# First half on one core: features as sixteen 32x32 tiles over head pairs, and a bias add that moves ahead of a norm's scaling

## The reference

```python
def favor(x, omega):                       # omega: 16 x 8
    xs = x * dh ** (-0.25)                 # dh = 16
    u = jnp.einsum('bshd,dm->bshm', xs, omega)
    h = 0.5 * jnp.sum(xs * xs, axis=-1, keepdims=True)
    return jnp.concatenate([jnp.exp(u - h), jnp.exp(-u - h)], axis=-1) * m ** (-0.5)
...
q, k, v = (out @ W[l] + b[l] for each of q, k, v), in 16 heads of 16
Qf, Kf = favor(q, omega[l]), favor(k, omega[l])
a = causal_linear_attention(Qf, Kf, v) @ Wo[l] + bo[l]
h = layer_norm(out + a, ln1_g[l], ln1_b[l])
y = relu(h @ W1[l] + bf1[l]) @ W2[l] + bf2[l]
out = layer_norm(h + y, ln2_g[l], ln2_b[l])
```

## Time and profile before

| what | value |
|---|---|
| median of the runs | 2623.1 us (3 runs, 2620.6 to 2625.83) |
| the profiled execution | 2624.48 us, its span 2622.7 us |
| PE, share of the span busy | 97% |
| DVE, ACT, POOL | 81%, 59%, 54% |
| mean granted clock of TensorE | 0.993 |
| largest step of the chain that ended last | PE, 90% |

### The profile page before, as it was taken

How to read it: one execution, slowest core, us unless ns; L and a number is a source line. 1 busy time by engine, 2 the same in 40 slices (tenths; PEclk the granted TensorE clock), 3 DMA queues, 4 the chain that set the end, 5 groups by cost and what they waited for, 6 DMA issues and landing times.

```text
span 2622.7 us, 63564 instructions
## 1 busy us (share of the span) xinstructions
PE 2545.6 (97%) x22368; PEld 2096.2 (80%) x22368; DVE 2119.8 (81%) x5244; ACT 1545.4 (59%) x3137; POOL 1423.9 (54%) x1406
## 2 busy tenths in 40 slices
PE   7899999999999999999898999999999999999998
PEld 4688888888888888887776788888888887888876
DVE  5788877887777787888899888878898887888775
ACT  3544455445544554455246777777777777776772
POOL 2244344443444345445476756656676666776664
PEclk9999999999999999999999999999999999999999
DMA  3100000010000010000111100000111100110001
GB/s 91 38 18 10 18 2 17 14 36 2 1 2 13 15 39 10 18 26 25 52 38 56 29 17 12 19 16 14 35 32 35 31 27 23 35 32 27 28 29 48
DMA packets 78985, 67.32 MB, mean 26 GB/s; under 512 B 15800, under 2 KB 73272, under 8 KB 78680
## 3 DMA queue, kind: packets, MB, share of 16 engines
q1 hardware_dynamic: 78680, 63.25, 8.1%
HBM read 49.18 MB, written 12.58 MB: 24 GB/s over the span
## 4 chain that ended last, share of the span: by engine, by line
PE 90%; DVE 4%; issue 3%; ACT 2%; POOL 1%; SPq 0%; DMA 0%; DVEq 0%; ACTq 0%; POOLq 0%
PE PS L274 79%; PE PS L984 4%; PE PS L946 1%; PE PS L1014 1%; PE PS L937 1%; PE PS L487 1%; PE PS L477 1%; PE PS L425 1%; PE PS L895 1%; DVE PS L3586 1%; DVE U L3178 1%; PE PS L1044 0%; ACT PR L2246 0%; DVE SQ L3566 0%; SPq L5388 0%
## 5 line engine op out<-in xcount | busy, mean ns | idle before, releaser
L2246 ACT ACTIVATE PR<-PS,SM 128x256 f32<-128x256 f32 (+1 forms) x512 | 280.3, 559 | 136.5 <-DVE SM L3591 136.0
L1932 ACT ACTIVATE FB<-PS,BC 128x512 f32<-128x512 f32 x192 | 133.4, 695 | 323.0 <-PE PS L274 184.7
L3178 DVE TENSOR_TENSOR U<-PS,CST 128x512 f32<-128x512 f32 x384 | 238.2, 683 | 34.2 <-PE PS L274 33.9
L4618 POOL TENSOR_TENSOR RL<-FB,RH 128x512 fp32r<-128x512 f32 x96 | 126.0, 1312 | 219.9 <-DVE RH L3155 219.9
L274 PE MATMUL PS<-W2H,RH 128*128 128x256 f32 x768 | 226.1, 294 | 6.7 <-POOL RL L4618 6.6
L4840 POOL TENSOR_TENSOR SM<-SM,COL 128x8 f32<-128x8 f32 x128 | 223.8, 1748 | 10.7
L3586 DVE CUSTOM_DVE_ANT_0 PS<-PS,MSK 128x256 f32<-128x256 f32 (+1 forms) x512 | 202.6, 436 | 29.4 <-PE PS L274 28.2
L274 PE MATMUL PS<-W2H,RL 128*128 128x256 f32 x768 | 215.9, 281 | 0.0
L274 PE MATMUL PS<-W2L,RH 128*128 128x256 f32 x768 | 215.8, 281 | 0.0
L4630 POOL TENSOR_TENSOR SBD<-SBD,TMP 128x256 f32<-128x256 f32 x84 | 64.3, 766 | 207.3 <-DVE TMP L3170 207.3
L274 PEld LDWEIGHTS PS<-W2H,RH 128*128 128x128 f32 x768 | 145.1, 189 | 29.5 <-issue 24.9
(11 more groups left out here) (265 smaller groups left out, 8535.6 us busy)
## 6 DMA issues: line engine op xcount, KB each, us to landing
PX<-in_L_attn_x SPq DMA_DIRECT2D x16, 512.0 KB, 3.6
TB<-in_k_rot SPq DMA_DIRECT2D x64, 128.0 KB, 2.1
SG<-in_L_attn_W SPq DMA_DIRECT2D x24, 256.0 KB, 2.7
xp_scratch<-PX SPq DMA_DIRECT2D x8, 512.0 KB, 2.9
xs_scratch<-X SPq DMA_DIRECT2D x64, 64.0 KB, 1.5
ZS<-xs_scratch SPq DMA_DIRECT2D x16, 256.0 KB, 2.8
GG<-xp_scratch SPq DMA_DIRECT2D x7, 512.0 KB, 3.8
out<-GG SPq DMA_DIRECT2D x7, 512.0 KB, 2.9
```

What stands on the lines that cost most here:

```text
L1932: e.activation(FB[:, hb % 2, :], PS[:, 5, :], ACT.Relu, bias=BC[:, l % 2, 4 + hb:5 + hb]).then_inc(*a_re.up(n, hb))
L2246: t = e.activation(PR[:, par, 256 * i + lo:256 * i + hi], PS[:, 3 + par, 256 * i + lo:256 * i + hi], ACT.Exp, bias=S[:, 40 + 2 * g + i:41 ...
L3178: e.tensor_tensor(heads(U[:, u % 6, :], 4), heads(PS[:, g, :], 4), bcast(CM, 4), ALU.mult).then_inc(*d_mk.up(n, u))
L4618: e.tensor_tensor(RL[:, r, :], FB[:, 0, :], RH[:, r, :].bitcast(F), ALU.subtract).then_inc(*p_rl.up(n, hb))
```

## The change

**Columns.** The 16 heads are dealt out over the projected tiles in pairs. Each of the four tiles now holds, in its four groups of 32 partitions, a pair of heads of the keys or the queries, so that `proj(n, i)` needs the weights of both and splits of them are written with a stride. **Operands.** ACT writes the columns with their bias to one full tile and the squares to another, with two activations of 128 x 512 for each i. **Visit.** `favor(n)` is one visit of 32 matmuls of 32 rows x 32 columns x 512: for each bank r and each operand c one with the omega weights, and then for each r and c one with the constant weights of the squares that adds to it. Rows 32r to 32r+31 of operand c go to partitions 32c to 32c+31 of bank r. It waits for all four operands and for both `add_bv(n, 0)` and `add_bv(n, 1)`. **Order.** On PE `values(n, 1)` moves ahead of `up(m, 2)` and `down(m, 1)`; on DVE `add_bv(n, 1)` moves ahead of `norm2_b(n - 3)` (in the stages 22 and 23 the order on DVE stays). **Loads.** The bias columns take four transfers instead of two per layer, `features_of` one operation of 128x32 instead of two of 128x128. `load_scales(0)` moves on SP ahead of the last loads of the first half, `load_scales(1)` to the start of the second half, and `table(u)` waits for the first six transfers alone while u < 32. For this GG, G0 and QSB lie elsewhere in SBUF.

```diff
         def proj(n, i):
-            m, nm = i % 2, "wk" if i < 2 else "wq"
...
-            need_weights(e, piece_of(n // 8, nm))
+            if i == 0:
+                need_weights(e, piece_of(n // 8, "wq"))
+                need_weights(e, piece_of(n // 8, "wk"))
...
-        def favor(n, i, bank):
+        def favor(n):
             l = n // 8
-            e.wait_ge(*p_om.at(l, 1))
-            e.wait_ge(*a_sq.at(n, i))
-            if i < 2:
-                e.wait_ge(*a_sq.at(n, 2 + i))
-            else:
-                e.wait_ge(*d_v.at(n, i - 2))
-            mm(e, PS[0:64, bank, :], OM[:, l % 2, 0:64], OPS[i][0], True)
-            mm(e, PS[64:128, bank, :], OM[:, l % 2, 64:128], OPS[i][1], True).then_inc(*e_fv.up(n, i))
+            e.wait_ge(*p_om.at(l))
+            for i in range(4):
+                e.wait_ge(*a_sq.at(n, i))
+            for i in range(2):
+                e.wait_ge(*d_v.at(n, i))
+            for r in BANKS:
+                for c in range(4):
+                    mm(e, PS[32 * c:32 * c + 32, r, :], OM[32 * r:32 * r + 32, l % 2, 0:32], OPS[c][0][32 * r:32 * r + 32, :], True)
+            for i, r in enumerate(BANKS):
+                for c in range(4):
+                    t = mm(e, PS[32 * c:32 * c + 32, r, :], HO[32 * r:32 * r + 32, 0:32], OPS[c][1][32 * r:32 * r + 32, :], False)
+                t.then_inc(*e_fv.up(n, i))
...
             values(n, 0)
             down(m, 0)
+            values(n, 1)
             up(m, 2)
             down(m, 1)
-            values(n, 1)
-            favor(n, 0, 2)
-            favor(n, 1, 3)
-            favor(n, 2, 0)
-            favor(n, 3, 1)
+            favor(n)
...
         def operands(n, i):
...
-            e.activation(A[lo, :], PS[lo, i, :], ACT.Identity, bias=col[lo, :])
-            e.activation(B[hi, :], PS[hi, i, :], ACT.Identity, bias=col[hi, :])
-            e.activation(A[hi, :], PS[lo, i, :], ACT.Square, bias=col[lo, :])
-            e.activation(B[lo, :], PS[hi, i, :], ACT.Square, bias=col[hi, :]).then_inc(*a_sq.up(n, i))
+            e.activation(A, PS[:, i, :], ACT.Identity, bias=col)
+            e.activation(B, PS[:, i, :], ACT.Square, bias=col).then_inc(*a_sq.up(n, i))
...
             splits(n, "v")
+            add_bv(n, 1)
             if z >= 0: norm2_b(z)
-            add_bv(n, 1)
...
+            if n < 23 and m >= 0: norm2_c(m)
             if n < 23: add_bv(n + 1, 0)
-            if n < 23 and m >= 0: norm2_c(m)
...
-                e.wait_ge(*t_qs.at(11))
+                e.wait_ge(*t_qs.at(11 if u >= 32 else 5))
```

More of the change, by code:

```diff
@@ L89, in build @@
     TB = sb("TB", [128, 2, 256])
-    QSB = sb("QSB", [128, 2, 256])
+    G0 = sb("G0", [128, 512])
     MSK = sb("MSK", [128, 384])
@@ L111, in build @@
     HTH, HTL = sb("HTH", [128, 2, 512], FR), sb("HTL", [128, 2, 512], FR)
-    GG = sb("GG", [128, 6, 512])
+    GG = sb("GG", [128, 5, 512])
+    QSB = sb("QSB", [128, 2, 256])
     PS = ctx.enter_context(nc.psum_tensor("PS", [128, 8, 512], F))
@@ L218, in build @@
     s_row = [ev(f"s_row{i}", by(range(3)), 16) for i in range(7)]
-    s_bb = ev("s_bb", by(range(3), range(11)), 16)
+    s_bb = ev("s_bb", by(range(3), range(13)), 16)
     s_x = ev("s_x", [("p", c) for c in S8] + [("r", n) for n in CH3], 16)
@@ L344, in split_parts, with places @@
         s = staged(p, n)
+        if phase == 1 and at < 1024:
+            def places(w, k):
+                return w[:, 512 * k:512 * k + 512].rearrange("p (s t m f) -> p t m s f", s=4, t=2, m=2)[:, at // 512, :, :, :]
+            return [(places(WQH, k), places(WQL, k), s[:, 256 * k:256 * k + 256].rearrange("p (m s f) -> p m s f", m=2, s=4)) for k in range(2)]
         if phase == 1:
@@ L614, in _ @@
         values(0, 0)
+        values(0, 1)
         modulate(4)
         modulate(5)
[L617 to L621, removed]
+        favor(0)
         turn_k(0, 0)
@@ L710, in _ @@
         values(3, 0)
+        values(3, 1)
         up(1, 2)
[L712 to L716, removed]
+        favor(3)
         up(1, 3)
@@ L3356, in _ @@
         modulate_b(4)
-        norm2_b(0)
         splits(3, "v")
@@ L3360, in _ @@
         add_bv(3, 1)
+        norm2_b(0)
         running(3, 0)
@@ L3444, in _ @@
         modulate_b(6)
-        norm2_b(2)
         splits(5, "v")
@@ L3449, in _ @@
         add_bv(5, 1)
+        norm2_b(2)
         running(5, 0)
@@ L5363, in store_scaled, with load_scales @@
             e.dma_start(xp_d[4 * c:4 * c + 4].rearrange("t p d -> p t d"), PX.rearrange("p i (t d) -> p (i t) d", t=2)).then_inc(*s_xp.up(n))
+        def load_scales(l):
+            for i, nm in enumerate(("q", "k")):
+                v = ins[f"L0_ffn_{nm}_scale"][l:l + 1, :]
+                for z, (a, b, n) in enumerate(((0, 0, 64), (64, 32, 32), (96, 0, 32))):
+                    e.dma_start(QSB[:, 1 - l, 128 * i + a:128 * i + a + n], v[:, b:b + n].broadcast_to([128, n])).then_inc(*t_qs.up(6 * l + 3 * i + z))
+        load_scales(0)
         for n in range(16, 21):
@@ L5510, in constants @@
     sign = np.where(i % 16 < 8, 0.5, -0.5).astype(f)
-    other = (((i[:, None] + 64) % 128) // 16 == i[None, :] // 16).astype(f) * f(-0.125)
-    cst = np.stack([np.eye(128, dtype=f), blk, other, (i[:, None] <= i[None, :]).astype(f), blk * sign[None, :]], axis=1)
+    pairs = (i[:, None] % 32 // 16 == i[None, :] % 32 // 16).astype(f)
+    cst = np.stack([np.eye(128, dtype=f), blk, pairs * f(-0.125), (i[:, None] <= i[None, :]).astype(f), pairs * sign[None, :]], axis=1)
     c = np.arange(32)
```

76 lines of the change are left out of this document (26 added, 50 removed).

## The result

The changed kernel takes 2608.05 us (median of 4 runs, 2605.81 to 2610.37) beside 2621.85 for the kernel before (4 runs): a ratio of 0.9945 with a 95% interval of 0.9928 to 0.9962, 14 us faster. The forecast was 2584 us, 39 us faster. The time lies inside the stated range of 2568 to 2610 and outside the forecast's own range of 2572 to 2600; the direction is right, and the size is off by almost a factor of three.

What follows compares the result with a forecast made beforehand. PE was taken to bound the stage loop, 53.0 us a turn. Gains of 28.2 + 0.9 + 3.3 - 0.7 - 0.3 + 7.5 = 38.9 us from 2624.48 gave 2585.6, median 2584 us; own range 2572 to 2600, stated range 2568 to 2610.

Steps and rivals of the forecast that it cites:

- 4 x 0.437 + 0.12 + 0.10 = 1.97: New visit's length in us: four rounds of sixteen sub-arrays, staggered starts, tile switch; own range used 1.75 to 2.3.
- The new wait at `up(m, 4)`: In each loop turn PE would wait about 0.2 us for ACT to free bank 5; 0 to 0.9 possible.
- What the visit waits for: Step on the visit's operands and both biases: no wait in the loop, edits at zero, covered by idle DVE and ACT.
- a sign of being wrong: Listed check in the profile after: PE waiting for the bias add in the loop would show the forecast wrong.
- My rival with the bias as the bound: Exponentials or bias bound the loop: waits of 0.9 us a stage, gain 0.7 instead of 1.41, about 2598 us; chance 0.11.
- stage 2: Visit there would wait for its bias add, losing about 0.5 us of the gain; net +0.9 us.
- the 0.9 of the forecast: Stage 23: the visit would wait 0.9 us for the bias adds, with DVE full behind it; net put at -0.3 us.
- Stage 1: Half the operands would end PE's 2.35 us wait for ACT; first scores about 3.3 us earlier, bounds 1.6 and 5.
- What waits for the visit: Step on the work behind the visit: banks ready together at its end, new wait 0.2 us, loop gain 1.41 per stage.
- The border: Between the halves: earlier scales shorten PE's 6.64 us stall and keep the clock up; 7.5 us gained, bounds 3 and 9.6.
- Start and stage 0: Strided weight splits on POOL and two more small DMAs: put at -0.7 us, bounds 0 and -2.5.
- The four-wide rival: Only four sub-arrays at a time: visit 7.1 us instead of 3.58 in 24 stages, some 2700 us; chance 0.08.

Runs made afterwards that it cites:

- experiments 4 and 5: Changed kernel with each visit's sixteen omega matmuls done twice: 2630.82 us, 1.0019; changed kernel without the four omega matmuls of bank 1: 2602.75 us, run once.
- experiment 6: Changed kernel with the visit's same 32 matmuls reordered, omega and squares of banks 2 and 3 first, then banks 0 and 1: 2622.71 us, 0.9989.
- Experiment 1: Changed kernel with DVE's second bias adds moved ahead of the work before them: 2600.64 us, 0.991; run once more: 2594.1 us, 0.9874.
- experiment 8: Changed kernel with bias adds first, table load first, and a down behind the visit in stages 4 and 5: 2596.51 us, 0.9881; again 2597.48 us.

## Why the prediction was wrong

**The mechanism of the visit was right, its size was off.** Sixteen sub-arrays did run side by side, in four rounds. The term "4 x 0.437 + 0.12 + 0.10 = 1.97" measured 2.28: 0.19 more for the late entry of the second sixteen and 0.15 for their wider spacing (fifteen steps of 17 ns instead of 7), with 0.03 less in the rest (experiments 4 and 5). Over twenty turns that is 6.2 us. Neither the bound of 1.75 nor the 2.3 of my range was passed.

**The new wait at `up(m, 4)`** was forecast at about 0.2 and is 0.19; experiment 6 showed it by taking it away. For a turn 1.30 - 0.19 = 1.11 is left, and the undisturbed turns are 1.11 to 1.20 shorter.

**The step that failed is "What the visit waits for".** It said of the operands and biases "no wait" and put the edits "at zero", on rows of stage 11 alone, one turn of the loop. It was right for that turn (the loop's turns other than 10 and 18 have no such wait) and wrong as a rule; PE waiting for the bias add in the loop had been named as a sign of being wrong, and these two stages are it: the list ahead of the add isn't the same in every stage. In stages 10 and 18 the weights' splitting stands there (2.05 us and about 0.9), in stage 1 `modulate_b(2)` (5.33), in stage 23 the norms (3.00, where I had put 0.9). I had named the condition myself, the cover being DVE's idle time, and had not gone through the stages in which DVE has other work. My rival with the bias as the bound had put that wait into every turn, at 0.9 us; it came in four single stages instead, at up to 5.33, beside the 0.53 of stage 2, which had been forecast at 0.5. Experiment 1 gives some 10 us of the 25 missed back. That includes the clock, which in these executions was 0.65 behind a 2 us wait in stage 10.

**The work ahead of the adds had also become longer.** The four scalings that took 3.71 us in stage 23 and 3.57 us in stage 1 had each taken 1.66 us in the kernel before. The rows are the norm of stage 23 before, then POOL beside it now, and POOL now in stages 1 and 10:

```profile
1238.77 1.66 DVE L3024 SCALAR_TENSOR_TENSOR PX<-Z,ST,PX 128x256 f32<-128x256 f32 x4
...
1225.22 2.87 POOL L4601 TENSOR_TENSOR X0L<-NUM,X0H 128x512 fp32r<-128x512 f32 x2 [1.16 <-ACT X0H L1927]
...
74.90 1.26 POOL L4601 TENSOR_TENSOR X0L<-NUM,X0H 128x512 fp32r<-128x512 f32 x1 [6.25 <-ACT X0H L1927]
76.57 1.39 POOL L4601 TENSOR_TENSOR X0L<-NUM,X0H 128x512 fp32r<-128x512 f32 x1 [0.41 <-ACT X0H L1927]
...
547.14 2.96 POOL L4601 TENSOR_TENSOR X0L<-NUM,X0H 128x512 fp32r<-128x512 f32 x2
```

In all three places single DVE operations that started while POOL's splitting ran took 1.4 to 1.8 us instead of 0.42 to 0.69, and in stage 1 both slow ones ended 0.28 us after POOL's did. The bias adds themselves, which read PSUM, kept their 0.41 us each. An estimate from these rows: with the old durations stage 23's wait would be 3.00 - 2.05 = 0.95, which is the 0.9 of the forecast, and the splits of stages 10 and 18, 2.2 and 1.1 us longer than before, would have cost no wait. In experiments 4, 5 and 6, whose order on DVE is the changed kernel's, `modulate_b(2)` ran ahead of POOL's splitting and took 1.66 us, and the wait of stage 1 was 2.24 us for ACT's operand. From experiment 6:

```profile
72.53 1.66 DVE L3006 SCALAR_TENSOR_TENSOR X<-PX,ST,MOD 128x256 f32<-128x256 f32 x4
...
73.87 1.44 POOL L4602 TENSOR_TENSOR X0L<-NUM,X0H 128x512 fp32r<-128x512 f32 x1 [7.88 <-ACT X0H L1928]
...
75.32 0.62 PE L276 MATMUL PS<-U,OM 32*32 32x512 f32 x3 [2.24 <-ACT KS L1888]
```

So the prediction's zero lacked two things, the order in the single stages and durations that depend on what POOL does at that moment. Experiment 1 shows that the order alone is enough to remove the waits. POOL's part is read from the times; no run took its work away.

**Stage 1** was forecast at +3.3 with the operands' wait gone. It didn't go: with the bias first, PE still waits 2.24 us for ACT's last operand (experiment 1), and in the changed kernel the later bias hides that wait. The first scores, foreseen at 84 to 85, start at 84.2 with the bias first and at 90.8 in the changed kernel.

**Stages 4 and 5** I had counted as turns of the loop. Their visit is followed directly by the output projection, which waits 0.84 us, and in stage 5 by the turned keys with another 0.83. The kernel before had neither wait. `attn_out` writes bank 2 and waits by the code for the first exponential, which reads that bank. In the old visit bank 2 was ready first, and the exponential began at 290.24 while the visit ran until 292.70; now it begins at 292.16, behind the visit, and the projection starts at 293.16. In experiment 6, where banks 2 and 3 are done first, the projection follows the visit without idle time. "What waits for the visit" had said that all banks come at the end and had followed that to `up(m, 4)` alone. The two turns together took 105.2 us instead of 105.0, with 2.8 less forecast: 3 us of the miss; experiment 8's traces show 1.4 of it coming back.

**The border** was forecast at 7.5 and gave 3.9 (1.8 to 6.3), near the lower bound of 3. The table landed 7.2 us after its issue, not 6.1, the table's and the splitting's steps behind it were 2.4 us, and PE waited 2.18 where I had put 0 to 1.4. The clock from 1275 to 1280 was 0.66, where I had named "above 0.9" as the sign. Both vary: in the eight traces with the new loads and the table's load in its old place the wait is between 0.53 and 2.32 us, and in the changed kernel's repetition it was 0.80 with the clock at 1.00 over the same stretch. I chose a value near the ceiling although the second half with its full DVE had been named against it; from the start of visit 23 to one and the same matmul behind the border (1325.83 before, 1309.66 after) the traces show 79.4 us instead of 85.0, of which 0.4 is the visit; from there to the end of the span the changed kernel takes 1298.8 us instead of 1296.9, so 1.9 of the 5.1 are given back.

**Start and stage 0** were put at 0.7 us slower and came 0.4 us faster in these traces; the next stretch varied by more than that between executions, so I don't read it.

**A small slip in a rival.** The four-wide rival is said to turn the sign from a visit of about 3.9 us on; with its own 11 us gained elsewhere that would be 11/24 or 0.46 above 3.58, about 4.0. Nothing hangs on it, since the visit measured 2.28 us.

What stays open: why groups of runs of one kernel differ by 0.3%. The granted clock of the runs (0.988 to 0.996) goes with it, and the stretch from visit 0 to visit 1 took between 45.3 and 48.8 us for kernels with the same code there; which of the waits in the first 80 us tips the clock I didn't separate.

## What to carry to other kernels

When a change turns four waits into one for all, go through every stage in which that wait occurs, and read in each what stands ahead of its producer on that engine; a turn of the loop in which it works shows nothing about the turn that has a weight load in it. The length of an operation in one place is not its length in another: look at what runs beside it. Moving the producer ahead of such work cost nothing here and gave 10 us, where the change itself had given 14 to 22. Before an operation is moved up, or its results come all at once, look at who reuses the buffer that it reads, not only at who reads its result.

## What the runs showed of the hardware

Sixteen 32x32 fp32 matmuls of 512 columns ran at once, sixteen starts within 0.10 us and a second record each 0.45 us later; the first records of all sixteen start before the second record of the first in the changed kernel. At most seventeen were under way: the eighteenth started 1.08 us after the first, on a busy or an idle sub-array, in the changed kernel and in experiments 4, 5 and 6. "TensorE: Matmul & The Clock Gate" in the Trainium skill, Part 3, says that matmuls start in program order; in experiment 6 the seventeenth started at 0.64 us, ahead of the ninth to the sixteenth (0.88 us on), and the measurement decides. The same 32 matmuls took 2.28 or 3.03 us by their order alone.

A DVE operation with all operands in SBUF that starts while POOL splits a tile of 128 x 512 ends after POOL's does: in the first half of the changed kernel's trace 29 scalings X<-Z of 128 x 256, 0.47 us otherwise, took 1.50 us in the median there, and every one ended 0.28 us behind POOL's operation. Those that read PSUM keep their length: ten bias adds beside the same splitting took 0.41 to 0.42 us each.
